# Gathering tokens in quarter rows and turning them on VectorE, in a gated attention and expert-FFN kernel

## What is computed

```python
def xattn(Q, K, V):                                        # Q: (8, 256, 512), K = V = ctx
    score = sigmoid(einsum('bdn,bdm->bnm', Q, K) / sqrt(256))
    return einsum('bvn,bnm->bvm', V, score)
def ffn(x):                                                # x: 2048 tokens x 512
    t = x * rsqrt(mean(x * x) + eps) * norm_w
    vals, idx = top_k(t @ gate_w.T + gate_b, 4)            # of 16 experts
    gates = softmax(vals)                                  # G: gates at idx, else 0
    h = einsum('mh,eoh->emo', t, w1) + b1
    a, b = minimum(h[..., ::2], 7), clip(h[..., 1::2], -7, 7)
    y = einsum('emi,edi->emd', a * sigmoid(1.702 * a) * (b + 1), w2) + b2
    return x + einsum('me,emd->md', G, y)
x = x + tanh(g_xattn) * xattn(layernorm(x), ctx, ctx)
x = x + tanh(g_ffn) * ffn(layernorm(x))
```

## Time and profile before

| | us |
|---|---|
| median of 3 runs | 850.59 (849.66 to 852.15) |
| the profiled execution, its own time | 851.6 |
| its span (first to last instruction) | 849.8 |
| TensorE busy | 780.2 (92%) |
| VectorE busy | 504.1 (59%) |
| ScalarE busy | 445.9 (52%) |
| GpSimd busy | 311.3 (37%) |
| granted TensorE clock, mean | 0.964 of full |

### The profile page before, as it was taken

One profiled execution on the slowest core, in us unless ns is written; L12 is line 12 of the kernel. 1 busy time (PEld: TensorE's weight loads), 2 busy tenths in 40 slices (PEclk: granted clock), 3 DMA queues, 4 the chain that ended last, 5 costly groups with the idle time before them and its releaser, 6 DMA issues.

```text
span 849.8 us, 16473 instructions
## 1 busy us (share of the span) xinstructions
PE 780.2 (92%) x3972; PEld 651.1 (77%) x3973; DVE 504.1 (59%) x1006; ACT 445.9 (52%) x771; POOL 311.3 (37%) x290
## 2 busy tenths in 40 slices
PE   5999998248999999999999999999999999999984
PEld 2544554237888899988889888899998988898873
DVE  2677666415676665566576664756557575746540
ACT  3445533115566575556557655646556565646540
POOL 0157575730433325233324323334333333325212
PEclk9999999559999999999999999999999999999997
DMA  8565654051586576348558654556535554544212
GB/s 288 177 198 176 230 163 111 20 139 51 125 229 145 125 214 165 58 138 208 123 163 212 173 114 131 148 136 148 148 57 151 107 150 131 156 123 74 37 25 38
DMA packets 107766, 116.98 MB, mean 138 GB/s; under 512 B 11808, under 2 KB 77344, under 8 KB 107744
## 3 DMA queue, kind: packets, MB, share of 16 engines
q1 hardware_dynamic: 88896, 77.32, 29.3%
q0 software_dynamic: 18848, 39.40, 23.6%
HBM read 88.06 MB, written 28.94 MB: 138 GB/s over the span
## 4 chain that ended last, share of the span: by engine, by line
PE 80%; DVE 7%; issue 7%; ACT 3%; DMA 1%; POOL 0%; DVEq 0%; ACTq 0%; POOLq 0%; SPq 0%; another core or an unknown queue 0%
PE ps L525 37%; PE ps L474 25%; PE ps L378 7%; PE ps L389 6%; PE ps L453 3%; DVE W1l L1028 1%; DVE uu L1017 1%; PE ps L406 1%; DVE hv L1019 1%; DVE bv L1015 1%; ACT hTh L698 1%; ACT bw L678 1%; PE ps L397 1%; ACT sg L675 1%; DVE ps L988 1%
## 5 line engine op out<-in xcount | busy, mean ns | idle before, releaser
L525 PE MATMUL ps<-xTh,W1h 128*128 x768 | 260.7, 339 | 10.2 <-issue 6.9
L525 PE MATMUL ps<-xTh,W1l 128*128 x768 | 255.0, 332 | 0.0
L525 PE MATMUL ps<-xTl,W1h 128*128 x768 | 255.0, 332 | 0.0
L1175 POOL DMA_INDIRECT out<-ys,dgI x75 | 118.8, 1584 | 309.2 <-ACT ys L657 285.2
L525 PEld LDWEIGHTS ps<-xTh,W1h 128*128 128x128 f32 x768 | 145.9, 190 | 20.4 <-issue 15.3
L525 PEld LDWEIGHTS ps<-xTh,W1l 128*128 128x128 f32 x768 | 145.8, 190 | 5.4
L525 PEld LDWEIGHTS ps<-xTl,W1h 128*128 128x128 f32 x768 | 146.0, 190 | 5.1
L474 PE MATMUL ps<-W2h,hTh 128*128 x300 | 120.3, 401 | 5.6 <-DVE hTl L1023 5.6
L474 PE MATMUL ps<-W2l,hTh 128*128 x300 | 118.1, 394 | 0.0
L474 PE MATMUL ps<-W2h,hTl 128*128 x300 | 117.9, 393 | 0.0
L657 ACT ACTIVATE ys<-ps,dgI 128x512 f32<-128x512 f32 x75 | 51.7, 689 | 124.2 <-DVE ps L988 120.2
(11 more groups left out here) (130 smaller groups left out, 995.4 us busy)
## 6 DMA issues: line engine op xcount, KB each, us to landing
W1f<-in_wts SPq DMA_DIRECT2D x64, 512.0 KB
W2f<-in_wts SPq DMA_DIRECT2D x32, 512.0 KB
X<-in_x SPq DMA_DIRECT2D x8, 512.0 KB, 6.3
Kt<-in_ctx SPq DMA_DIRECT2D x8, 512.0 KB
Vt<-in_ctxT SPq DMA_DIRECT2D x8, 512.0 KB
rows<-tt SPq DMA_DIRECT2D x8, 512.0 KB
out<-base SPq DMA_DIRECT2D x8, 512.0 KB
b2s<-in_bias SPq DMA_DIRECT2D x16, 256.0 KB
```

The costliest lines, as they stand in the source:

```text
L525: m = e.matmul(P_[i % 2][:, 0:64 * w], (W1h, W1l)[wl][:, i, 2 * k + h, :], (xTh, xTl)[xl][:, bass.ds(par, 1), k, 0:64 * w], start=(t == 0) ...
L1175: e.indirect_dma_start(out, bass.IndirectOffsetOnAxis(dgI[:, j, 0:1].bitcast(I32), axis=0), ys[j][:], None, compute_op=ALU.add).then_inc(d ...
```

## The change

- `rows` holds the values of a token in another order: `centred` writes value c * 128 + m at place 4 * m + c. `gwT` is loaded in the matching order, by four DMAs in place of one.
- A tile of 128 tokens is gathered by four indirect DMAs. Piece i takes tokens 32 i to 32 i + 31; partition quarter q receives quarter q (512 bytes) of each row: 128 descriptors of 512 bytes for each DMA.
- The index lists for this are built once: 16 SP transfers copy `idx` from SBUF to SBUF (`idx4`, 32 partitions of 2312 bytes each), between the loads of `idx` and the last base store, behind waits for both loads; one GpSimd `tensor_scalar` over 4 x 289 elements makes row numbers (`row4`). `place` copies 16 elements (`src4`) in place of 8.
- VectorE turns a tile with one `transpose` of 32x32 blocks, 128x512, from `xg[i]` into `PX`: `turn(0)` ahead of `hidden(0)`, `turn(1)` ahead of `second()`, `turn(2)` behind `turned_in(1)`, `turn(3)` behind `hidden(1)` and `turned_in(2)`. TensorE no longer turns tiles in the loop.
- The first unit's four tiles are gathered whole, into `ys[j]`, and turned by TensorE as before.
- ScalarE keeps the gates of the unit before in `gcur` itself, and waits for the scatters (`d_s`) itself (`added_back`); it holds six fields of a unit in place of four.

```diff
+            e.wait_ge(d_idx0, 16)
+            e.wait_ge(d_idx, 16)
+            for i in range(4):
+                for q in range(4):
+                    e.dma_start(idx4[32 * q:32 * q + 32, i, 0:(E + 1) * TE, :], idx[32 * i:32 * i + 32, 0:(E + 1) * TE, :]).then_inc(d_idx4, 16)
             store_base(B - 1)
...
-                    if i == 0:
-                        turned_in(0)
-                        second_layer(e.snap(u * 4 + 4))
-                    if i < 3:
-                        turned_in(i + 1)
...
-                e.scalar_tensor_tensor(tt[b % 2][:, j, :], x1[b % 2][:, j, :], mv1[:, b, j, 0:1], nwb[:], ALU.subtract, ALU.mult).then_inc(v_u, 1)
+                e.scalar_tensor_tensor(tt[b % 2][:, j, :].rearrange("p (m c) -> p c m", c=4), x1[b % 2][:, j, :].rearrange("p (c m) -> p c m", c=4),
+                                       mv1[:, b, j, 0:1], nwb[:].rearrange("p (c m) -> p c m", c=4), ALU.subtract, ALU.mult).then_inc(v_u, 1)
...
+            def added_back():
+                with e.If(e.snap(done, min_val=0, max_val=NTILES) > 0):
+                    e.wait_ge(d_s, e.snap(e.snap(done, min_val=1, max_val=NTILES) * 16))
+                    e.sem_inc(e_ga, 1)
...
+                def turn(i):
+                    with e.If(more > LESS[i]):
+                        e.reg_add(landed[i], landed[i], 64)
+                        e.wait_ge(d_g[i], e.snap(landed[i], min_val=64, max_val=64 * NTILES))
+                        e.wait_ge(e_xl, e.snap(e.snap(split, min_val=4, max_val=NTILES + 24) + 1))
+                        e.transpose(PX[:].rearrange("p (i c t) -> p i c t", i=4, c=4), xg[i][:].rearrange("p (i s c) -> p i c s", i=4, c=4)).then_inc(e_tx, 1)
...
+                turn(0)
                 by_width(lambda w: hidden(0, w))
                 turned_in(0)
+                turn(1)
                 second()
                 turned_in(1)
+                turn(2)
...
             def gather(j):
-                e.indirect_dma_start(xg[j][:], None, rows, bass.IndirectOffsetOnAxis(srcI[:, j, 0:1].bitcast(I32), axis=0)).then_inc(d_g[j], 16)
+                for i in range(4):
+                    e.indirect_dma_start(xg[j][:, 128 * i:128 * i + 128], None, rows.rearrange("r (q h) -> (r q) h", q=4),
+                                         bass.IndirectOffsetOnAxis(src4[:, j, i:i + 1], axis=0)).then_inc(d_g[j], 16)
...
+            e.wait_ge(d_idx4, 256)
+            e.tensor_scalar(row4[:, :, 0:(E + 1) * TE], idx4[:, :, 0:(E + 1) * TE, 0].bitcast(I32), 4.0, C[:, C_PIECE:C_PIECE + 1], op0=ALU.mult, op1=ALU.add).then_inc(e_src, 1)
```

More of the change, by code:

```diff
@@ L113, in build @@
         hTl = sb("hTl", [128, 4, H], F32R)
-        sb("ph", [128, 2, C2 // 2])
+        idx4 = sb("idx4", [128, 4, (E + 1) * TE + 3, 2])
+        row4 = sb("row4", [128, 4, (E + 1) * TE + 3], I32)
+        assert sb.place[0] <= hT_at + 16 * 4 * H
+        sb.place[0] = hT_at + 16 * 4 * H
         ys_at = sb.place[0]
@@ L216, in build @@
         d_b, d_b1 = sem("d_b"), sem("d_b1")
-        d_idx0, d_idx, d_s = sem("d_idx0"), sem("d_idx"), sem("d_s")
+        d_idx0, d_idx, d_idx4, d_s = sem("d_idx0"), sem("d_idx"), sem("d_idx4"), sem("d_s")
         d_g = [sem(f"d_g{j}") for j in range(4)]
+        d_first = [sem(f"d_first{j}") for j in range(4)]
         e_src, e_dg = sem("e_src"), sem("e_dg")
@@ L304, in sp @@
             e.dma_start(nwb[:], nw.partition_broadcast(128)).then_inc(d_cc, 16)
-            e.dma_start(gwT[:], gw).then_inc(d_cc, 16)
+            for c in range(4):
+                e.dma_start(gwT[c:128:4, :, :], gw.rearrange("(q s) c e -> c s q e", q=4)[c]).then_inc(d_cc, 16)
             e.dma_start(gbb[:], gb.partition_broadcast(128)).then_inc(d_cc, 16)
@@ L500, in pe @@
                 wide = e.snap(now[F_HL], min_val=1, max_val=8)
[L501 to L508, removed]
                 ready = e.snap(e.snap(turned, min_val=4, max_val=NTILES + 24) + 1)
@@ L549, in pe @@
                     e.reg_mov(a, q)
+                e.reg_add(turned, turned, now[F_NT])
+                with e.If(e.snap(now[F_NT], min_val=0, max_val=4) < 2):
+                    e.reg_add(turned, turned, 1)
                 load_fields(e, nxt, e.snap(u + 2), 0)
@@ L648, in act, with keep_gates @@
             e.reg_mov(done, 0)
-            e.reg_mov(was[F_NT], 0)
-            e.reg_mov(was[F_LAST], 0)
+            for r in was:
+                e.reg_mov(r, 0)
             load_fields(e, now, 0, 0)
             load_fields(e, nxt, 1, 0)
+            def keep_gates():
+                row = e.snap(was[F_ROW], min_val=0, max_val=(E + 1) * TE - 1)
+                e.copy(gcur[:], idx[:, bass.ds(row, 4), 1:2]).then_inc(e_bc, 1)
+            def added_back():
+                with e.If(e.snap(done, min_val=0, max_val=NTILES) > 0):
+                    e.wait_ge(d_s, e.snap(e.snap(done, min_val=1, max_val=NTILES) * 16))
+                    e.sem_inc(e_ga, 1)
             def gated(j):
@@ L967, in dve @@
             was, now, nxt = many_regs(e, "dve_was", 4), many_regs(e, "dve_now", 4), many_regs(e, "dve_nxt", 4)
+            landed = many_regs(e, "dve_landed", 4)
             split, done = e.alloc_register("dve_split"), e.alloc_register("dve_done")
+            for r in landed:
+                e.reg_mov(r, 0)
             e.reg_mov(split, 4)
@@ L1055, in pairs @@
                             turned_in(i + 1)
+                        if i == 1:
+                            turn(3)
                         low_h(i, w)
@@ L1124, in pool @@
             e.wait_ge(d_zrow, 16)
-            place(0, 1)
+            e.wait_ge(a_base, 2 * B)
+            e.tensor_copy(srcI[:], idx[:, 0:4, :]).then_inc(e_src, 1)
+            e.wait_ge(e_src, 1)
             for j in range(4):
-                gather(j)
+                e.indirect_dma_start(ys[j][:], None, rows, bass.IndirectOffsetOnAxis(srcI[:, j, 0:1].bitcast(I32), axis=0)).then_inc(d_first[j], 16)
             e.wait_ge(v_te, 3)
-            e.wait_ge(d_idx, 16)
+            e.wait_ge(d_idx4, 256)
+            e.tensor_scalar(row4[:, :, 0:(E + 1) * TE], idx4[:, :, 0:(E + 1) * TE, 0].bitcast(I32), 4.0, C[:, C_PIECE:C_PIECE + 1], op0=ALU.mult, op1=ALU.add).then_inc(e_src, 1)
+            e.wait_ge(e_src, 2)
             n = units(e)
@@ L1152, in gathers @@
                         gather(j)
-            e.wait_ge(e_tx, 4)
-            place(row(nxt), 2)
+            place(row(nxt), 3)
             gathers(nxt)
@@ L1181, in pool @@
                 e.sem_inc(e_go, 1)
-                place(row(fut), e.snap(u + 3))
+                place(row(fut), e.snap(u + 4))
                 gathers(fut)
```

63 lines of the change are left out of this document (38 added, 25 removed).

## The result

933.52 us (median of 4 runs, 927.35 to 940.33) against 850.79 (849.66 to 852.15) of the kernel before on the same chip: ratio 1.097, 95% interval 1.087 to 1.107. The change costs 83 us where a gain of 10 was forecast. The profiled execution took 940.33 us, with a span of 938.6. All ratios here are of fast runs alone, since some executions fall into a slower state, while medians are of all runs; in runs 2, 4 and 11 the two therefore differ a little.

A forecast was written before the change was run, and what follows sets the result against it. TensorE was taken as the bound, with 80% of the chain. Terms -24.6 + 4 + 6 + 3.3 + 1 = -10.3 us gave 840.3 us; the forecast's own range was 830 to 847, the whole range 828 to 866.

The forecast's parts named there:

- GpSimd's gathers: Loop: four pieces a tile, each priced as a whole gather, bring GpSimd level with TensorE and VectorE; +6 us, range 0 to +34.
- TensorE's turns: Loop: 71 of 75 tiles no longer turned on TensorE; -24.6 us, with 0 as the lower end.
- VectorE's, +4: Loop: 71 transposes at 0.7 us delay five or six stretches where TensorE waits for VectorE; +4 us, +7 at 1.2 us each.
- the start: Start of stage 2: index copies delay the first part by 8.8 us, partly regained behind it; +3.3 us net, range 0 to +8.
- the rest: Three more SP issues at the start, one ScalarE copy and four register moves a turn of the loop; +1 us.
- GpSimd's pitch: Loop: time from one gather to the next on GpSimd, taken as 1.47 us, bounds 1.25 and 1.9.
- GpSimd becomes the bound: Rival, chance 0.28: in the loop the pitch passes 1.53 us; at 1.6 the kernel takes 866 us.
- The rule on VectorE's and GpSimd's shared interfaces: Loop: VectorE instructions with two SBUF inputs or two-port mode slow GpSimd's gathers; one took 1.93 us against 0.95 alone.
- What holds up next: Loop: VectorE's turns wait for late pieces with its other work queued behind, then ScalarE and TensorE wait; within the +6 us.
- The sum: Whole kernel: all terms add to -10.3 us, giving a forecast median of 840.3 us.

The follow-up runs named there:

- run 2: The kernel before with four 512-byte gathers a tile in place of one, TensorE still turning the tiles: 1011.19 us, ratio 1.176.
- run 4: The changed kernel with each tile's four gathers taking 32 whole 2048-byte rows, VectorE turning: 1017.98 us, ratio 1.196.
- run 11: The changed kernel with the last base store issued ahead of the index wait and the sixteen index copies: 929.64 us, ratio 1.088.
- run 1: Also called whole_gathers: the changed kernel with one whole-row gather a tile in place of four pieces, VectorE still turning: 848.66 us, ratio 0.9955.
- run 18: run 16 with the last eight gathers of each unit's row cut from 512 to 32 bytes a token: 978.31 us, ratio 1.145.
- run 9: The changed kernel with a small GpSimd memset, not waited for, behind each tile's four gathers: 935.99 us, ratio 1.101.
- run 10: The changed kernel with one waited-for memset a unit of four tiles, behind the second tile's pieces: 912.66 us, ratio 1.072.
- run 12: The changed kernel with two 1,024-byte gathers a tile in place of four of 512 bytes: 861.17 us, ratio 1.011.
- run 16: run 15 with 512 bytes a token in place of 32 in the unread gathers, written into `tt`: 980.01 us, ratio 1.147.
- run 17: run 15 with each tile's three small gathers ahead of its whole-row gather, not behind all four: 980.35 us, ratio 1.145.
- run 15: run 1 with twelve unread gathers of 32 bytes a token added behind each unit's four whole-row gathers: 848.07 us, ratio 1.0015.
- run 5: The changed kernel with a small GpSimd memset and a wait for it behind each tile's four pieces: 928.07 us, ratio 1.096.
- run 8: The changed kernel, base store first, each tile's pieces issued once its buffer is turned, scatters between tiles 1 and 2: 868.53 us, ratio 1.0275.
- run 7: run 1 with the last base store issued ahead of the index copies and their waits: 839.41 us, ratio 0.9926.
- run 13: The kernel with four whole-row gathers a unit, then ten small waited-for GpSimd memsets a tile, no added gathers: 846.12 us, ratio 1.001.

## Why the prediction was wrong

The step that failed is the one on **GpSimd's gathers**, and not in its arithmetic: it priced a row of 16 gathers by its length alone, on GpSimd, charged +6 us for it, and let everything else on the chip run on beside it. The runs show another cost. On the chip of the change and on chips 5, 7 and 15, TensorE's completions reach ScalarE and VectorE up to 14 us late beside rows of 8 to 16 gathers, and the engines wait for them: 63 us in the change, with a loss of 83.

The evidence is made of comparisons on one chip. On chip 7 the loss follows the rows of pieces with either turning engine (runs 1, 2), grows while GpSimd idles more and nobody waits for a piece (run 4), and comes with gathers that nobody reads (run 18 against run 1: 127 us, 137 us of remote waits). On chip 15 an operation of another kind between the gathers changes nothing (run 9), a waited-for break every eight helps by a quarter (run 10), and rows of at most eight in all leave 7.9 us of remote waits (run 12).

What is not settled is what else it takes. Runs 16, 17 and 18 differ from run 15 in the bytes, the order or the place of the unread data, and none of these by itself explains all four; the sort of chip does, since runs 16 to 18 are on chips 5 and 7 and run 15 on chip 2. That is the simplest reading and it was not tested: it needs run 15 on chip 7, or run 18 on chip 2. For the same reason runs 5 and 8 do not show that a break every four gathers ends the hold, and how the change would do on chips 2, 11 or 12 is open. Nor do the traces show by what mechanism a signal is held. That the recording of raises is itself at work, since it is incomplete on just the chips with late signals, is not excluded. The waits are real in the traces, and all four timed runs of the change are long.

Point by point:
- *TensorE's turns, -24.6; VectorE's, +4.* The transposes take 1.109 us, not 0.7. This is near the 1.2 that the prediction estimated from the Trainium skill (VectorE: DVE Perf Modes, The three transpose paths); +7 would have been the term. The page's price is for a bf16 block that goes to SBUF and this is float32 into PSUM, so the agreement can be luck. VectorE is no bound (62% of the span). In whole_gathers, which has both of these and the start, the sum is -4 (0.45%) where these terms and the rest give -24.6 + 7 + 3.3 + 1 = -13. With the store first it is -6.6. Which of the terms is short by the 9 us was not measured apart.
- *GpSimd's pitch.* Forecast 1.47, measured 1.48; GpSimd busy 550.5 us, forecast 560. +6 was charged for it. Without late signals, as much GpSimd time costs 5 us where the added gathers are wanted by nobody (run 15) and 29 where the pieces are wanted and spread (run 8 against run 7), so the size was right only for the easy case. The forecast's reason, that a gather's time is the writing of its 128 descriptors, fits badly: 32 rows a gather still take 0.87 us at the median, against 0.96. The rival "GpSimd becomes the bound" had the sign and not the mechanism: the mean pitch stayed under its 1.53, and GpSimd still waits 126 us for `ys`.
- *The rule on VectorE's and GpSimd's shared interfaces* (the Trainium skill, GPSIMD Engine Reference, Specifications). The change's trace agrees. All 46 gathers over 1.4 us (up to 2.03) run beside VectorE's `low_w` or `low_h`, and gathers beside these take 1.30 us on the mean, the others 0.98. Over all pieces the mean is 1.125, less than the 1.17 of the forecast, so the rule does not reach the loss.
- *The start.* A copy takes 0.63 us on SP and not 0.42 (16 in 10.09 us), with the store landing 3.06 us after its issue and not 6.3. From the first index transfer to TensorE's first part it is now 24.9 us (168.27 to 193.15) against 13.9 before: +11.0, forecast +8.8. The second part follows the first without a stop, as forecast:
```profile
172.14 0.59 SPq L364
...
182.27 3.06 DMA out<-base
...
193.15 13.72 PE ps L528 x48
```
(the chain of waits after). At the end of the second part the delay is 206.87 - 168.27 = 38.6 against 33.0, +5.6, forecast +4.8 before the 1.5 for the turns was taken off.
- *What holds up next.* That VectorE would wait behind late pieces did not come about (24.3 us in all). The late signals reach `add_bias` and ScalarE's gates instead, then `ys`, and through `ys` both TensorE's tile 3 and GpSimd's scatters, so the next row starts later as well.
- *The sum.* The forecast left +93 us unexplained. Of that, some 9 are the smaller gain of run 1, and 5 to 29 are GpSimd's time by runs 15 and 8, measured on chips without late signals. Some 55 to 79 remain for the late signals, an estimate by difference. The 63 us of remote waits seen on three engines fit it, but overlap only in part.

## What to carry to other kernels

Splitting one indirect gather into four costs GpSimd four times the instruction (a median of 0.87 us for 32 rows of 2,048 bytes, and 0.95 for 128 rows of 32 or 512 bytes). What is worse, the longer rows can delay engines that have nothing to do with it. Issue gathers a few at a time between other work; look for "remote" waits in or just behind rows of another engine's gathers. When engines off the chain are loaded further, test that load alone, with data nobody reads, before the rest of the change is built. Test it together with its control on one chip, and on more than one: here twelve such gathers a unit cost 5 us on one chip and some 127 on another. Stage 1 of any of these traces tells which sort of chip it was taken on.

## What was not expected of the hardware

- Completions of TensorE come up to 14 us late beside rows of GpSimd gathers, when hand-overs between VectorE and ScalarE take under 0.9 us.
- This is seen on the change's chip and on chips 5, 7 and 15 (15 to 69 late raises in the loop, in the kernels whose rows are longer than four gathers), and not on chips 2, 11 and 12, of which chip 2 ran rows of 12 and 16 gathers. On the former, 18% to 24% of the raises of stage 1 have no record.
- A GpSimd memset of 0.13 us in the row changes nothing; with a wait behind it, 0.91 us of pause, one every eight gathers takes a quarter of the loss and leaves raises up to 12.3 us late. One every four gathers was run only on a chip without late signals.
- A wait at the end of GpSimd's row also exposes 2.2 us of register loading a unit (47 to 48 us in all) that otherwise lies under the queued gathers. In run 13 it costs nothing.
- A 128x512 fp32 transpose by VectorE into PSUM takes 1.09 to 1.14 us.
- A 32-partition SBUF-to-SBUF copy costs SP 0.63 us of issue.
